# The negative maxima are issued ahead of the query and key stacks on SyncE's queue

## The chip, the cores and the metric

One core of a Trainium2 chip runs the kernel. The metric is the device time of one execution in microseconds (us); less is better. The median of three runs is shown together with the lowest and highest.

## The reference

An input x of 8 sequences of 1,024 positions by 256 channels goes through one attention layer with 16 heads of 16 channels, in which a query sees only itself and the 128 positions before it, and then through a linear layer whose weights are replaced by their signs. Both have a layer norm (without gain) ahead and a residual around them.

```python
def attn(x):                                   # x is the layer norm of the input
    q = (x @ Wq.T + bq).reshape(B, S, 16, 16)  # k and v the same way
    scores = einsum('bqhd,bkhd->bhqk', q, k) * 0.25
    scores = where((j <= i) & (j >= i - 128), scores, -10000.0)
    p = softmax(scores, axis=-1) + 1e-9
    return einsum('bhqk,bkhd->bqhd', p, v).reshape(B, S, 256) @ Wo.T + bo
x = x + attn(layernorm(x))
x = x + layernorm(x) @ sign(weight).T
```

## The kernel before

Each of the 8 sequences is cut into 8 tiles of 128 positions, and two tiles make a pair. One slot of the main loop handles one tile's scores, and beside them, in software pipelining, other steps for tiles ahead and behind; `parts(b, t)` (L201) says which: `nm` is two tiles ahead, `mx` three ahead, `xr` two behind, `op` three behind, `ff` four behind; `k` (in even slots) is the pair that starts four tiles ahead, `ks` (in odd slots) the pair that starts one tile ahead. There are 64 slots and four short ones behind them. Below, "slot 24" is the 24th from 0, and t is its number within its sequence (slot 24 has t = 0, slot 25 has t = 1).

For the softmax the kernel finds an upper bound for each query row and head with cheap bf16 products: `max_scores` (L986) multiplies `q_stack` by `k_max` on TensorE into the tile `mx`, `row_max` (L716) reduces it on VectorE into `nmax` (negated), `turn_max` (L1019) transposes that on TensorE, `nmax_part` (L552, L558) copies it on ScalarE to `nmax_t`, and `stack_nmax` (L285) sends it by DMA into two rows of `q_stack`, where it is multiplied by a row of ones in `k_stack` and so is subtracted from the scores. `scores` (L1027) is the fp32 product of `k_stack` and `q_stack`, in 8 groups f of two heads (L1050), and `exp` (L536) takes the exponentials on ScalarE.

The stacks are built by DMAs inside SBUF, all on SyncE's queue: `stack_q` (L243) sends a pair's queries in six DMAs of 128 KB (parts hi, hi, lo, each for two row groups, L256), `stack_k` (L269) a pair's keys in six DMAs of 128 KB (L282), `set_k_max` (L259) the bf16 keys in two DMAs of 64 KB (L266). `load_xr` (L292) fetches the residual's input and waits for `x2_done` of the slot before, `load_x` (L237) a pair of input tiles, and the output goes out at L317.

What waits for these DMAs on TensorE, which works in its own fixed order:

- `scores(b, t, 0)` waits for `nmax_stacked` of tile t + 1 (at t = 0 of tiles 0 and 1; at t = 7 of none), in even slots also for `k_stacked` of the slot's pair.
- `max_scores(..., 0)` waits, for an even tile, for `q_headed` (the first two query DMAs) and `k_max_set` (both of L266) of its pair. This tile is three ahead, so the wait falls into odd slots, one slot after the DMAs were issued.

In an odd slot TensorE's order is: `turn_max`, `scores` f = 0, `t1` (where there is a pair), `turn_u`, `turn_x2`, `scores` f = 1, then `max_scores` 0, and the rest. In an even slot SyncE's order is `load_xr`, `stack_q` three times, `stack_nmax`, `set_k_max`, output; in an odd slot `load_xr`, `stack_k`, `stack_nmax`, `load_x`, output. `stack_nmax` waits for `nm_done`, which L558 sets. `set_k_max` waits for `k_16_done`, the bf16 copy of the keys on ScalarE.

Of the kernel before, what the change touches and what calls it, by code (L numbers as in the profile page):

```python
# [45 lines left out]
def build(nc, x, wq_t, wk_t, wv_t, wo_t, wf_t, bq_c, bk_c, bv_c, bo_r, out):  # L46
# [7 lines left out]
    with ExitStack() as ctx:  # L54
# [132 lines left out]
        def wait(eng, s, n):  # L187

            if n > 0:
                eng.wait_ge(s, n)  # L190

        def halves(t):


            return t % 2, t // 2
# [5 lines left out]
        def parts(b, t):  # L201

            def tile(shift):
                bb, tt = b + (t + shift) // TILES, (t + shift) % TILES
                if not 0 <= bb <= LAST:
                    return None
                return bb, tt

            def pair(shift):
                n = t + shift  # L210
                if n % 2:
                    return None
                bb, pp = b + n // TILES, n // 2 % PAIRS
                if not 0 <= bb <= LAST:
                    return None
                return bb, pp

            if b > LAST:
                now = None
            else:  # L220
                now = (b, t)
            return now, {"nm": tile(2), "mx": tile(3), "pv": tile(-1), "xr": tile(-2), "op": tile(-3), "ff": tile(-4),
                         "tqv": pair(5), "k": pair(4), "ks": pair(1), "ln": pair(6), "load": pair(7)}

        def run(eng, slot):

            for b in range(BATCHES):
                for t in range(TILES):
                    slot(b, t)
            for t in range(4):  # L230
                slot(BATCHES, t)
# [3 lines left out]
        @block.sync  # L235
        def _(sp):
            def load_x(b, p):  # L237
                i, n = halves(p)

                wait(sp, xn_done, PAIRS * b + p - 1)  # L240
                sp.dma_start(xs[:, i], x_pair[b, p]).then_inc(x_loaded[i], 16)

            def stack_q(b, p, r):  # L243
                i, _ = halves(p)
                cols = slice(2 * P * p, 2 * P * (p + 1))
                g = PAIRS * b + p
                src = (q_hi, q_hi, q_lo)[r]
                stacked = q_stacked[i] if r else q_headed[i]

                wait(sp, sc_filled, SC_FILLS * (TILES * (b - 1) + 2 * p + 2))  # L250
                if g < PAIRS:
                    sp.wait_ge(q_zeroed, 1 if g == 0 else 2)
                sp.wait_ge(q_lo_done if r == 2 else q_hi_done, g + 1)
                for c in range(C):
                    at = 64 * c + DK * r
                    sp.dma_start(q_stack[at:at + DK, :, cols].bitcast(F32),  # L256
                                 src[:, g % 2, c, :].bitcast(F32)).then_inc(stacked, 16)

            def set_k_max(b, p):  # L259
                i, _ = halves(p)  # L260
                g = PAIRS * b + p

                wait(sp, mx_filled, MXG * (TILES * (b - 1) + min(2 * p + 3, TILES)))
                sp.wait_ge(k_16_done, g + 1)
                for c in range(C):
                    sp.dma_start(k_max[64 * c:64 * c + DK, :, P + 2 * P * p:P + 2 * P * (p + 1)],  # L266
                                 k_16[:, c, :]).then_inc(k_max_set[i], 16)

            def stack_k(b, p):  # L269
                i, _ = halves(p)  # L270
                g = PAIRS * b + p
                cols = slice(2 * P * (g % 2), 2 * P * (g % 2 + 1))

                wait(sp, sc_filled, SC_FILLS * (2 * g - 2))
                if g < 2:
                    sp.wait_ge(k_zeroed, g + 1)
                sp.wait_ge(k_hi_done, g + 1)
                sp.wait_ge(k_lo_done, g + 1)
                for c in range(C):
                    for r, src in enumerate((k_hi, k_lo, k_hi)):  # L280
                        at = 64 * c + DK * r
                        sp.dma_start(k_stack[at:at + DK, HB * c:HB * (c + 1), cols].bitcast(F32),  # L282
                                     src[:, g % 2, c, :].bitcast(F32)).then_inc(k_stacked[i], 16)

            def stack_nmax(b, t):  # L285
                i, _ = halves(t)
                sp.wait_ge(nm_done, TILES * b + t + 1)
                at = 3 * DK
                sp.dma_start(q_stack[at:at + 65:64, :, P * t:P * (t + 1)].bitcast(F32),
                             nmax_t[:, i, :].bitcast(F32)).then_inc(nmax_stacked[i], 16)  # L290

            def load_xr(b, t):  # L292
                i, _ = halves(t)

                wait(sp, x2_done, TILES * b + t - 1)
                sp.dma_start(xr[:, i], x_tile[b, t]).then_inc(xr_loaded[i], 16)

            def slot(b, t):
                now, part = parts(b, t)
                if part["xr"]:  # L300
                    load_xr(*part["xr"])
                if part["k"]:
                    for r in range(3):
                        stack_q(*part["k"], r)
                if part["ks"]:
                    stack_k(*part["ks"])
                if part["nm"]:
                    stack_nmax(*part["nm"])
                if part["load"]:
                    load_x(*part["load"])  # L310
                if part["k"]:
                    set_k_max(*part["k"])
                if part["ff"]:
                    bb, tt = part["ff"]
                    i, _ = halves(tt)
                    sp.wait_ge(y_done, TILES * bb + tt + 1)
                    sp.dma_start(y_tile[bb, tt], x2[:, i]).then_inc(y_stored[i], 16)  # L317

            def stack_ones(i):

                sp.wait_ge(k_zeroed, i + 1)
                for c in range(C):
                    at = 64 * c + 3 * DK
                    sp.dma_start(k_stack[at:at + 1, HB * c:HB * (c + 1), 2 * P * i:2 * P * (i + 1)].bitcast(F32),
                                 ones[0:HB, :]).then_inc(ones_stacked[i], 16)

            load_x(0, 0)
            load_x(0, 1)
            for dst, src in ((bq, bq_c), (bk, bk_c), (bv, bv_c), (bo, bo_r)):
                sp.dma_start(dst[:, :], src).then_inc(b_loaded, 16)  # L330
            load_x(0, 2)
            stack_q(0, 0, 0)
            stack_q(0, 0, 1)
            set_k_max(0, 0)
            stack_q(0, 0, 2)
            sp.wait_ge(ones_done, 1)
            stack_ones(0)
            stack_k(0, 0)
            stack_q(0, 1, 0)
            set_k_max(0, 1)  # L340
            stack_nmax(0, 0)
            stack_q(0, 1, 1)
            stack_nmax(0, 1)
            stack_q(0, 1, 2)
            load_x(0, 3)
            stack_ones(1)
            run(sp, slot)
            for i in range(2):
                sp.wait_ge(y_stored[i], 16 * (NT // 2))
# [984 lines left out]
```

## Time and profile before

| | us |
|---|---|
| median of 3 runs | 728.42 |
| lowest and highest run | 723.81, 730.84 |
| profiled execution, its own time | 729.17 |
| its span in the trace | 727.4 |
| TensorE busy (PE) | 667.2 (92% of the span) |
| VectorE, ScalarE, GpSimd busy | 493.5, 484.9, 457.5 |
| SyncE's DMA queue, share of 16 engines | 63.0% |

All times in the trace are us from the start of the span. In a timeline a row gives start, length, engine, line and operation, the number of instructions merged in it, and in brackets the idle time before it with what ended it. PE is TensorE's matmuls, PEld its weight loads, SPq the DMA issues of SyncE. "DMA q_stack<-nmax_t" as the end of a wait means that the transfer's landing ended it; "issue" means that the profile shows nothing that did. In the table of DMA issues the last number is the median time from the start of the issue to the landing, where there is one.

### The profile page before, as it was taken

How to read it: one execution, taken by the hardware profiler on the slowest of the kernel's cores; microseconds unless marked ns; L12 is line 12 of the kernel's file. 1: busy time of each engine (PE TensorE's matmuls, PEld its weight loads, DVE VectorE, ACT ScalarE, POOL GpSimd, SP SyncE). 2: the span in 40 equal slices, each digit the busy share in tenths (PEclk: the TensorE clock that was granted, in tenths of full speed). 3: DMA queues.
4: the chain of work that ended last, by engine and by line, in shares of the span. 5: the costliest groups of instructions: out<-in, count | busy, mean ns of one | idle time of the engine just before them, and what ended most of it. 6: DMA issues, size and time to landing. Idle time of an engine off the chain costs nothing.

```text
span 727.4 us, 31464 instructions
## 1 busy us (share of the span) xinstructions
PE 667.2 (92%) x13076; PEld 593.4 (82%) x13076; DVE 493.5 (68%) x1043; ACT 484.9 (67%) x1061; POOL 457.5 (63%) x650
## 2 busy tenths in 40 slices
PE   4579999999999999999999999999999999998874
PEld 4468888888988988888998888889888889887663
DVE  4544777777777777787677777677777777766434
ACT  4346777776767666777767677686767777675631
POOL 7924467766666667656666676475667666566652
PEclk9767999999999999999999999999999999999999
DMA  4957477876777676775767767675686757665401
GB/s 140 118 79 114 91 125 134 133 126 110 123 134 127 114 123 127 136 121 107 129 129 129 111 130 121 105 133 111 115 139 118 135 113 124 127 111 99 74 30 37
DMA packets 94940, 83.73 MB, mean 115 GB/s; under 512 B 10416, under 2 KB 94800, under 8 KB 94800
## 3 DMA queue, kind: packets, MB, share of 16 engines
q1 hardware_dynamic: 93440, 80.42, 63.0%
q8 instruction: 104, 1.70, 1.3%
q10 hardware_dynamic: 1360, 1.31, 0.5%
q14 instruction: 36, 0.29, 0.2%
HBM read 18.22 MB, written 8.39 MB: 37 GB/s over the span
## 4 chain that ended last, share of the span: by engine, by line
PE 77%; DMA 7%; DVE 5%; SPq 4%; issue 4%; ACT 2%; POOL 1%; DVEq 0%; ACTq 0%; POOLq 0%
PE gc L916 17%; PE sc L1050 16%; PE ga L916 12%; PE pv L1066 12%; DMA q_stack<-nmax_t 6%; PE mx L1007 5%; PE mx L1013 4%; PE ga L1076 3%; SPq L256 3%; DVE nmax L724 3%; PE gc L931 2%; PE gb L1105 2%; PE gb L1088 2%; ACT prob L548 1%; DMA k_stack<-k_hi 1%
## 5 line engine op out<-in xcount | busy, mean ns | idle before, releaser
L548 ACT ACTIVATE prob<-sc 128x512 f32<-128x512 f32 x448 | 259.2, 598 | 99.2 <-PE sc L1050 95.4
L724 DVE TENSOR_REDUCE nmax<-mx 128x6 f32<-128x960 f32 x189 | 197.1, 1043 | 75.6 <-PE mx L1013 74.4
L1050 PE MATMUL sc<-q_stack,k_stack 128*128 128x256 f32 (+1 forms) x1024 | 210.2, 305 | 8.9 <-DMA q_stack<-nmax_t 4.6
L1050 PEld LDWEIGHTS sc<-q_stack,k_stack 128*128 128x128 f32 x1024 | 150.6, 191 | 24.0 <-DMA q_stack<-nmax_t 7.2
L432 POOL TENSOR_SCALAR ve<-mv 128x1 f32<-128x1 f32 x64 | 14.2, 222 | 215.5 <-DVE mv L796 213.9
L419 POOL TENSOR_SCALAR_AFFINE_SELECT prob<-prob 128x1024 f32<-128x1024 f32 x128 | 139.8, 1092 | 0.0
L416 POOL TENSOR_SCALAR_AFFINE_SELECT prob<-prob 128x1024 f32<-128x1024 f32 x112 | 122.3, 1092 | 17.8 <-ACT prob L548 17.8
L1066 PE MATMUL pv<-prob,v_ones 128*32 128x128 f32 x3840 | 120.2, 277 | 1.0 <-POOL prob L419 0.7
L1066 PEld LDWEIGHTS pv<-prob,v_ones 128*32 128x32 f32 x3840 | 102.3, 111 | 10.2 <-POOL prob L419 1.0
L1013 PE MATMUL mx<-k_max,q_stack 16*32 16x160 bf16 x4032 | 72.0, 231 | 5.2 <-issue 5.2
L762 DVE TENSOR_TENSOR ct_lo<-gb,ct_hi 128x256 fp32r<-128x256 f32 x64 | 26.9, 420 | 45.1 <-ACT ct_hi L565 44.7
L1007 PE MATMUL mx<-edges,ident 32*32 32x192 bf16 (+1 forms) x1328 | 44.9, 246 | 10.8 <-DVE nmax L724 6.1
L1013 PEld LDWEIGHTS mx<-k_max,q_stack 16*32 16x32 bf16 x4032 | 44.7, 91 | 7.5 <-issue 6.1
L1007 PEld LDWEIGHTS mx<-edges,ident 32*32 32x32 bf16 x1328 | 18.8, 88 | 37.3 <-issue 15.0
L784 DVE TENSOR_TENSOR x<-ga,xr 128x256 f32<-128x256 f32 x64 | 27.2, 425 | 30.6 <-PE ga L916 29.4
L427 POOL TENSOR_TENSOR xr<-xr,brow 128x256 f32<-128x256 f32 x64 | 46.9, 732 | 0.0
L408 POOL TENSOR_TENSOR vsum<-vsum,v_ones 128x256 f32<-128x256 f32 x56 | 41.1, 734 | 2.5
L579 ACT ACTIVATE u<-pv 128x512 f32<-128x512 f32 x64 | 38.9, 608 | 5.6 <-PE pv L1066 5.5
L550 ACT ACTIVATE prob<-sc 128x256 f32<-128x256 f32 x64 | 23.7, 387 | 28.4 <-PE sc L1050 28.4
L504 ACT ACTIVATE q_hi<-gc,bq 128x256 fp32r<-128x256 f32 x64 | 26.8, 470 | 19.4 <-PE gc L916 16.8
L1076 PE MATMUL ga<-ident,u 128*128 128x128 f32 x256 | 38.7, 273 | 0.8 <-DVE x L784 0.8
L434 POOL TENSOR_TENSOR rs<-ve,half 128x1 f32<-128x1 f32 x64 | 36.0, 563 | 5.3
(149 smaller groups left out, 1409.2 us busy)
## 6 DMA issues: line engine op xcount, KB each, us to landing
q_stack<-q_hi SPq DMA_DIRECT2D x128, 128.0 KB, 3.6
k_stack<-k_hi SPq DMA_DIRECT2D x128, 128.0 KB, 4.4
xs<-x SPq DMA_DIRECT2D x32, 256.0 KB, 4.5
q_stack<-q_lo SPq DMA_DIRECT2D x64, 128.0 KB
k_stack<-k_lo SPq DMA_DIRECT2D x64, 128.0 KB, 4.2
xr<-x SPq DMA_DIRECT2D x64, 128.0 KB, 2.0
out<-x SPq DMA_DIRECT2D x64, 128.0 KB, 2.1
k_max<-k SPq DMA_DIRECT2D x64, 64.0 KB, 3.4
```

The costliest lines, as they stand in the source:

```text
L408: g.tensor_tensor(s, s, v, ALU.add).then_inc(vsum_step, 1)
L416: g.affine_select(out=nxt, in_=nxt, compare_op=ALU.is_ge, fill=0.0, base=0, pattern=[[0, HB], [-1, P]], channel_multiplier=1)
L419: g.affine_select(out=own, in_=own, compare_op=ALU.is_ge, fill=0.0, base=0, pattern=[[0, HB], [1, P]], channel_multiplier=-1).then_inc(pro ...
L427: g.tensor_tensor(xr[:, i], xr[:, i], brow[:, :], ALU.add).then_inc(xb_done, 1)
L548: a.activation(prob[:, own:nxt + 1:nxt - own, 2 * f:2 * f + 2, :], sc, ACT.Exp, scale=SCALE).then_inc(exp_done, 1)
L724: v.tensor_reduce(nmax[:, n % 2, :].rearrange("p (r h) -> p r h", r=C)[:, :, h0:h0 + m], banks[:, :, 0:WIN * m].rearrange("p r (h k) -> p ...
L916: last = mm(dst, l, r, start=j == 0, stop=j == len(terms) - 1)
L1007: mm(dst, ident16[rows, rows], mask.unsqueeze(1).broadcast_to(list(dst.shape)), start=True, stop=False, skip_group_check=True)
L1013: last = mm(banks[QB * blk:QB * (blk + 1), rg, WIN * j:WIN * (j + 1)], q_16[64 * rg:64 * rg + DK, h, at:at + QB], k_max[64 * rg:64 * rg + ...
L1050: last = mm(sc_bank[f % 2][:, 2 * P * j:2 * P * j + q], k_stack[:, h, ak:ak + P], q_stack[:, h % HB, P * t:P * t + q], start=True, stop=True)
L1066: last = mm(pv_bank[32 * j:32 * (j + 1), P * cg:P * (cg + 1)], v_ones[:, tile, h, :], prob[:, part, h, :], start=cg == 0 and k == 0, stop= ...
L1076: last = nc.tensor.transpose(ga[:, P * cg:P * (cg + 1)], u[:, t % 2, P * cg:P * (cg + 1)], ident[:, :])
```

## The change

In `slot` of SyncE's program the call of `stack_nmax` moves from behind `stack_q` and `stack_k` to the place in front of them, behind `load_xr`. No instruction is added or removed, and the part ahead of the loop keeps its order.

```diff
                 if part["xr"]:
                     load_xr(*part["xr"])
+                if part["nm"]:
+                    stack_nmax(*part["nm"])
                 if part["k"]:
                     for r in range(3):
                         stack_q(*part["k"], r)
                 if part["ks"]:
                     stack_k(*part["ks"])
-                if part["nm"]:
-                    stack_nmax(*part["nm"])
                 if part["load"]:
                     load_x(*part["load"])
                 if part["k"]:
```

## Rows read from the trace of the kernel before

**Rows 1.** The page: busy time of the engines.
```profile
PE 667.2 (92%) x13076; PEld 593.4 (82%) x13076; DVE 493.5 (68%) x1043; ACT 484.9 (67%) x1061; POOL 457.5 (63%) x650
```
**Rows 2.** Waits: who waited for whom, total us, times, longest us.
```profile
PEld mx L1007 <- issue: 16.4, 61, 2.6
PEld sc L1050 <- DMA q_stack<-nmax_t: 7.2, 12, 1.0
```
**Rows 3.** Timeline, SyncE's DMA issues in slots 24 (even) and 25 (odd).
```profile
294.25 0.33 SPq L296 DMA_DIRECT2D xr<-x  x1
294.69 2.54 SPq L256 DMA_DIRECT2D q_stack<-q_hi  x4
297.32 1.20 SPq L256 DMA_DIRECT2D q_stack<-q_lo  x2
298.57 0.55 SPq L289 DMA_DIRECT2D q_stack<-nmax_t  x1
299.97 1.60 SPq L266 DMA_DIRECT2D k_max<-k  x2
...
302.95 0.34 SPq L296 DMA_DIRECT2D xr<-x  x1
303.40 0.57 SPq L282 DMA_DIRECT2D k_stack<-k_hi  x1
...
307.19 0.60 SPq L282 DMA_DIRECT2D k_stack<-k_hi  x1
307.84 0.55 SPq L289 DMA_DIRECT2D q_stack<-nmax_t  x1
```
**Rows 4.** Timeline, TensorE at the start of slot 25.
```profile
303.23 0.51 PE L1050 MATMUL sc<-q_stack,k_stack 128*128 128x256 f32 x2 [0.42 <-DMA q_stack<-nmax_t]
...
304.99 0.28 PE L1007 MATMUL mx<-edges,ident 32*32 32x192 bf16 x8
```
**Rows 5.** DMA issues at 303.40 and 307.19, the first and last key DMA: to landing.
```profile
k_stack<-k_hi SPq DMA_DIRECT2D x1, 128.0 KB, 3.2
...
k_stack<-k_hi SPq DMA_DIRECT2D x1, 128.0 KB, 4.7
```
**Rows 6.** DMA issues: the second k_max of slots 24, 38, 20, 2, in this order.
```profile
k_max<-k SPq DMA_DIRECT2D x1, 64.0 KB, 3.6
k_max<-k SPq DMA_DIRECT2D x1, 64.0 KB, 4.6
k_max<-k SPq DMA_DIRECT2D x1, 64.0 KB, 3.8
k_max<-k SPq DMA_DIRECT2D x1, 64.0 KB, 2.3
```
**Rows 7.** Timeline, slots 38 and 39 (t = 7): k_max issues, TensorE's mx.
```profile
446.47 1.19 SPq L266 DMA_DIRECT2D k_max<-k  x2
...
451.79 0.28 PE L1007 MATMUL mx<-edges,ident 32*32 32x192 bf16 x8 [1.02 <-issue]
```
**Rows 8.** Timeline, slot 7, the first with t = 7: TensorE's mx.
```profile
119.36 0.28 PE L1007 MATMUL mx<-edges,ident 32*32 32x192 bf16 x8 [0.29 <-issue]
```
**Rows 9.** Timeline, slots 20 and 21 (t = 5): k_max issues, TensorE.
```profile
258.87 1.20 SPq L266 DMA_DIRECT2D k_max<-k  x2
...
261.90 0.51 PE L1050 MATMUL sc<-q_stack,k_stack 128*128 128x256 f32 x2 [0.76 <-DMA q_stack<-nmax_t]
...
263.66 0.40 PE L1007 MATMUL mx<-window,ident 32*32 32x480 bf16 x8
```
**Rows 10.** Timeline, ScalarE's copies of the maxima in slots 2 and 25.
```profile
68.49 0.25 ACT L558 ACTIVATE nmax_t<-gb 16x128 fp32r<-16x128 f32 x1
...
303.23 0.25 ACT L558 ACTIVATE nmax_t<-gb 16x128 fp32r<-16x128 f32 x1
```
**Rows 11.** Timeline, slots 2 and 3: SyncE's issues, TensorE's mx.
```profile
63.95 2.83 SPq L256 DMA_DIRECT2D q_stack<-q_hi  x4
...
73.35 1.58 SPq L266 DMA_DIRECT2D k_max<-k  x2
...
78.37 0.28 PE L1007 MATMUL mx<-edges,ident 32*32 32x192 bf16 x8
```
**Rows 12.** Timeline, TensorE's first scores of slots 16 and 26.
```profile
211.00 0.71 PE L1050 MATMUL sc<-q_stack,k_stack 128*128 128x256 f32 x4 [0.37 <-DMA k_stack<-k_hi]
...
313.48 0.72 PE L1050 MATMUL sc<-q_stack,k_stack 128*128 128x256 f32 x4
```

## The prediction

> **What bounds the kernel now.** I read the page first: TensorE is busy for 92% of the span and no other engine for more than 68% [rows 1]. So a change pays if it takes idle time out of TensorE's order, and costs if it puts some in. The waits view comes next: TensorE's weight loads stood 7.2 us, in 12 longer waits, until a DMA of negative maxima had landed [rows 2]. These are the first scores of odd slots. Slot 25 shows one: the DMA is issued at 298.57, behind six query DMAs, and the scores start at 303.23, 4.66 us later [rows 3, 4]. Slots with t = 7 have no such wait in the program, and in even slots the maxima are issued 5.6 us ahead of their use (307.84, scores at 313.48 [rows 3, 12]). So 7.2 us is what this order costs at that place; it is what the change can take away.
>
> The second place to look at is the next thing that an odd slot waits for: `max_scores` 0, behind f = 1, waits for `k_max`, which stands at the end of the same queue. In slot 39 the second `k_max` DMA is issued at 446.47 + 0.60 = 447.07 and takes 4.6 us to land, 451.7; TensorE starts `mx` at 451.79 after 1.02 us idle, labelled "issue" [rows 6, 7]. That label hides a DMA wait. The same reading holds in 6 of the 7 slots with t = 7 from slot 7 on (the first idles 0.29 us [rows 8]): there `mx` starts within 0.1 us of the landing. In the slots in which the maxima's wait comes first, `mx` starts soon after `k_max` landed: slot 25 at 304.99 against 300.57 + 3.6 = 304.2, a margin of 0.8; slot 21 at 263.66 against 259.47 + 3.8 = 263.3, a margin of 0.4 [rows 3, 4, 6, 9].
>
> **The queue is bound by its transfers, not by its issues.** SyncE issues a 128 KB DMA every 0.6 to 0.75 us. The key DMAs of slot 25 land at 303.40 + 3.2 = 306.6 (first) and 307.19 + 4.7 = 311.9 (last) [rows 3, 5]: five more DMAs in 5.3 us, 1.05 us each, about 125 GB/s. The query chain does the same, and `k_max` comes at its end: 304.2, which is 9.5 us after the first query issue (the median over the sequence of slots, read in this way, is 9.65). With the queue empty `k_max` needs 2.3 us from its second issue (slot 2, where the queries had gone long before) [rows 6, 11]; in slot 24 it needs 3.6. It stands 1.3 us behind transfers, so its landing follows the start of the chain, not its own issue. The Trainium skill, SBUF — State Buffer, section on the DMA port swizzle, says that bandwidth goes by how many of the 16 ports the partitions reach; 16 destination partitions reach four, an estimate of 109 GB/s and 1.2 us for such a DMA. The trace's 1.05 us is near that.
>
> **The change, part by part.** Nothing is added or removed; one DMA moves past six.
>
> 1. The maxima's DMA in even slots. It takes 0.55 us to issue and about 0.07 to the next: 0.62. ScalarE's copy is done when `load_xr` has been issued in the even slots (0.5 us to spare), so it waits for nothing and lands some 2.5 us after the slot's start instead of in the next slot. The waits at f = 0 vanish: at most 7.2 us gained.
>
> 2. The query chain starts 0.62 us later, so `k_max` lands 0.62 us later. I take the full 0.62, from the 1.05 us per DMA; the bounds are 0 (if the chain were issue-bound, since `k_max` is issued as before) and 0.62. Per odd slot TensorE gains the smaller of its f = 0 stall and (margin of `mx` behind `k_max`, less 0.62), which can be negative. Slot 25: stall 0.63, margin 0.76, gain 0.14. Slot 21: stall 0.96, margin 0.31, a loss of 0.31. Summed in this way over the 28 odd slots 5 to 59, for the bound 0 and for 0.62:
>
> | slots with | f = 0 stalls | gain, shift 0 | gain, shift 0.62 |
> |---|---|---|---|
> | t = 1 (7 slots) | 1.5 | +1.5 | +0.4 |
> | t = 3 (7) | 0.7 | +0.7 | 0.0 |
> | t = 5 (7) | 5.0 | +3.4 | -0.8 |
> | t = 7 (7) | 0 | 0 | -4.0 |
>
> The last line is what matters: with t = 7 there is nothing to gain, and `k_max` is already the wait, so six slots pay 0.62 and one pays 0.24.
>
> 3. The key chain in odd slots starts 0.62 us later, and up to 0.5 more where ScalarE's copy comes late: in slot 25 it ends at 303.48, when the first key DMA was issued at 303.40 [rows 3, 10]. Queued behind that wait are the six key DMAs, `load_x` and the output. The late copies (0.5) are in slots with t = 3, whose key landings have 2.7 us in hand. Elsewhere it is thin: 1.6 us in slot 26 (311.9 against 313.48 [rows 3, 5, 12]), none in slot 16, where the scores already wait for a key DMA [rows 12], and none in slot 50. Less 0.62, and less what the slot before gained, this costs 0.9 us at shift 0.62 (slots 42 and 50) and 1.6 us at shift 0.
>
> 4. The start. In slot 2 the queries are issued at 63.95, while the maxima are ready at 68.74 [rows 10, 11]: the chain starts 5.4 us later, at 69.4, and `k_max` lands at 69.4 + 9.65 = 79.0, against `mx` at 78.37 [rows 11]: 0.7 us lost. The waits in slots 0, 1 and 3 are covered by margins above 1 us, but for slot 1's `mx`, by 0.5.
>
> Sum: +0.4 + 0.0 - 0.8 - 4.0 - 0.9 - 0.7 = -6.0, so 6.0 us slower. The profiled execution's own time is 729.17, so 735.2; it stands 0.75 above the median 728.42, and against the median it is 734.4.
>
> **The rivals.** (a) The chain isn't work-conserving: `k_max` lands when it did, because it is issued when it was. Then 5.6 us are gained at f = 0, 1.6 lost to keys, none at the start: -4.0, so 724.4. For it speaks that the two DMAs' issues don't move, and that in slots whose fifth query issue came a microsecond late, the queries still all landed 8.9 us after the first issue. Against it: those had a backlog before them, and landings 1.05 apart are a full queue. The whole of 7.2 would come only if `k_max` were also ahead; the margins of 0.3 to 0.8 exclude it. The Trainium skill, DMA: Bandwidth & Descriptors, Anatomy of one DMA, fits a DMA at 2.0 us plus bytes over 436 GB/s: an estimate of 0.3 us for each 128 KB, by which the chain would be issue-bound and this rival right. The 1.05 us speaks against that here. (b) The shift is about half, 0.3: the same sum gives 0.0, and with the start 0.7 slower, 729. (c) SyncE gets stuck: one more DMA is outstanding ahead of the queries, SyncE's long issues (1.58 and 1.60 for two [rows 3, 11]) multiply, and `k_max` and the keys come a further 0.15 us late. With 28 odd slots that is 4 us more, 738.5; it decides once `k_max` lands over 0.75 us later. (d) The change doesn't do what it says: the maxima still land late. Only a late ScalarE copy could do that, and it isn't late in even slots.
>
> **How the numbers follow.** Full shift, 734.4: 0.50. Rival (a): 0.25. (b): 0.15. (c): 0.08. (d) and others: 0.02. The likeliest by itself spans 731 to 737. The range for 8 in 10 takes in (b), (c) and the upper part of (a): 724 to 738.5. About 1%, 7.3 us, is what a measurement can tell from no change. Faster by more than that needs all of the 7.2 us: 0.03. Slower by more than that needs (c) or the upper third of the first case: 0.25. Within 1%: 0.72.
>
> **What would show it.** The waits of TensorE for the maxima's DMA vanish from odd slots' first scores. The idle time labelled "issue" ahead of L1007 at the first `mx` of odd slots grows by about as much and more, with `k_max` landing 10.1 to 10.3 us after the slot's first query issue would have been (9.5 to 9.7 after the issue itself). In slots with t = 7 that idle time is 0.6 longer. If `k_max` lands 9.0 us after the first query issue, rival (a) is right. A few first scores of even slots wait for key DMAs. The prediction is wrong if a gain shows at f = 0 and none of it is given back at `mx`.

## The result, and the profile after

| | before | changed |
|---|---|---|
| median of 12 runs each, us | 730.05 | 735.93 |
| lowest and highest | 723.81, 732.20 | 732.55, 741.51 |
| ratio, 95% interval | | 1.0115 (1.0087 to 1.0142) |
| profiled execution: its own time, span | 729.17, 727.4 | 741.51, 739.5 |

The changed kernel is 5.9 us slower by the medians and 8.4 by the ratio (0.0115 x 730). The profiled execution of the changed kernel happens to be the slowest of its twelve, so its span overstates the difference. A second profile of each kernel was therefore taken (below), and both stand in the tables of slots 4 to 59.

The page of the changed kernel: busy time of the engines. TensorE does the same work, 666 us, in a longer span; the difference is idle time, as in [rows 1].

```profile
PE 666.3 (90%) x13076; PEld 593.3 (80%) x13076; DVE 494.1 (67%) x1043; ACT 486.2 (66%) x1061; POOL 457.7 (62%) x650
```

Its waits (who waited for whom, total us, times, longest), to be set against [rows 2]. The 7.2 us for the maxima's DMA are gone. The idle time ahead of the first kind of `mx` matmul went from 16.4 to 32.0, and the idle time labelled "issue" ahead of the scores from 1.2 to 6.3.

```profile
PEld mx L1007 <- issue: 32.0, 71, 4.5
...
PEld sc L1050 <- issue: 6.3, 11, 1.0
```

The last of these in the kernel before:

```profile
PEld sc L1050 <- issue: 1.2, 4, 0.6
```

SyncE's issues in slots 24 and 25 of the changed kernel, the slots of [rows 3].

```profile
296.54 0.57 SPq L289 DMA_DIRECT2D q_stack<-nmax_t  x1
297.22 2.52 SPq L256 DMA_DIRECT2D q_stack<-q_hi  x4
299.84 1.20 SPq L256 DMA_DIRECT2D q_stack<-q_lo  x2
302.45 1.65 SPq L266 DMA_DIRECT2D k_max<-k  x2
...
305.44 0.34 SPq L296 DMA_DIRECT2D xr<-x  x1
305.99 0.57 SPq L289 DMA_DIRECT2D q_stack<-nmax_t  x1
306.67 0.57 SPq L282 DMA_DIRECT2D k_stack<-k_hi  x1
```

TensorE at the start of slots 25 and 26. The first scores of slot 25 (305.10) follow without a wait, where [rows 4] had 0.42 us. Those of slot 26 now wait: their keys were issued later.

```profile
305.10 0.48 PE L1050 MATMUL sc<-q_stack,k_stack 128*128 128x256 f32 x2
...
306.84 0.28 PE L1007 MATMUL mx<-edges,ident 32*32 32x192 bf16 x8
...
316.22 0.71 PE L1050 MATMUL sc<-q_stack,k_stack 128*128 128x256 f32 x4 [0.63 <-issue]
```

And a slot with t = 7, slot 39, with the second `k_max` issue of slot 38 (450.79) in the table of DMA issues: 450.79 + 4.6 = 455.4, and `mx` starts at 455.52 behind 1.01 us of idle time. That is no longer than before (1.02 [rows 7]): slot 38 is an exception. There `k_max` lands 11.70 us after the slot's start before the change and 11.69 after it. The second query DMA was issued 1.20 us behind the first before and 0.60 now (1.13 and 0.60 in the second profiles), so the chain had been late there already. Slot 7 shows the usual case: where [rows 8] had 0.29 us of idle time, the gap between weight loads is 0.88 us against 0.40 before.

```profile
455.52 0.27 PE L1007 MATMUL mx<-edges,ident 32*32 32x192 bf16 x8 [1.01 <-issue]
```
```profile
k_max<-k SPq DMA_DIRECT2D x1, 64.0 KB, 4.6
```

The same readings over all slots, from the issues, landings and weight loads of the traces. "Start" of a slot is the weight load of its `turn_max`; the medians are over slots 4 to 56 (27 even slots, or the odd ones behind them), in us. "2nd" is the second profile of the same kernel.

| | before | 2nd | changed | 2nd |
|---|---|---|---|---|
| first query issue behind the even slot's start | 1.18 | 1.18 | 1.79 | 1.79 |
| k_max landed, behind the first query issue | 9.66 | 9.61 | 9.62 | 9.69 |
| k_max landed, behind the even slot's start | 10.84 | 10.79 | 11.41 | 11.48 |
| first key issue behind the odd slot's start | 0.93 | 0.96 | 1.75 | 1.74 |
| keys landed, behind the first key issue | 8.65 | 8.73 | 8.88 | 8.88 |

And TensorE's idle time in slots 4 to 59, summed by place from gaps above 0.15 us ahead of the first weight load of each:

| us | before | 2nd | changed | 2nd |
|---|---|---|---|---|
| first scores, odd slots (maxima) | 7.2 | 7.2 | 0 | 0 |
| first mx, odd slots (k_max) | 3.1 | 3.4 | 13.9 | 14.0 |
| first scores, even slots (keys) | 0.8 | 1.1 | 4.5 | 3.9 |
| length of slots 4 to 59 | 580.6 | 579.6 | 587.5 | 585.2 |

The three places together grew by 7.3 and 6.2 us, the slots by 6.9 and 5.6. One thing beside the waits adds to the 6.9: in the first profile of the changed kernel TensorE's granted clock was at half for 3.4 us from 666.9 on, in slot 59, which lasts 12.4 us against 10.4 and 10.9 before and 11.0 in the second profile.

### The profile page after: what moved, and what is told of

It reads as the page before. It is cut to its first block, busy times and chain, and to the rows that moved or that the text cites. A ratio compares the mean times of both kernels' runs of the same rounds, so it can differ in the third digit from the quotient of the medians.

```text
span 739.5 us, 31464 instructions
## 1 busy us (share of the span) xinstructions
PE 666.3 (90%) x13076; PEld 593.3 (80%) x13076; DVE 494.1 (67%) x1043; ACT 486.2 (66%) x1061; POOL 457.7 (62%) x650
## 4 chain that ended last, share of the span: by engine, by line
PE 84%; issue 5%; DVE 4%; POOL 2%; ACT 2%; DMA 1%; SPq 1%; POOLq 0%; DVEq 0%; ACTq 0%
PE gc L916 18%; PE sc L1050 17%; PE pv L1066 15%; PE ga L916 13%; PE mx L1007 6%; PE mx L1013 5%; PE ga L1076 4%; DVE nmax L724 2%; PE gb L1105 2%; PE gb L1088 2%; PE gc L931 2%; DMA q_stack<-q_hi 1%; PE gb L1025 1%; SPq L282 1%; ACT prob L548 1%
## 5 line engine op out<-in xcount | busy, mean ns | idle before, releaser
L1066 PEld LDWEIGHTS pv<-prob,v_ones 128*32 128x32 f32 x3840 | 103.4, 112 | 10.5 <-issue 1.2
L1007 PE MATMUL mx<-edges,ident 32*32 32x192 bf16 (+1 forms) x1328 | 44.6, 244 | 20.1 <-issue 13.8
```

The lines of the kernel that those rows point to most:

```text
L1007: mm(dst, ident16[rows, rows], mask.unsqueeze(1).broadcast_to(list(dst.shape)), start=True, stop=False, skip_group_check=True)
L1066: last = mm(pv_bank[32 * j:32 * (j + 1), P * cg:P * (cg + 1)], v_ones[:, tile, h, :], prob[:, part, h, :], start=cg == 0 and k == 0, stop= ...
```

## The experiments

Each was timed in turns with the kernel before on the same chip; "of before" is the ratio with its 95% interval. Two theories are tested: H, the head of the chain of transfers (what is put ahead of the queries delays `k_max`, their last link), and rivals that put the cost elsewhere. All diffs are against the kernel before, in SyncE's `slot`, unless it is said otherwise.

### The change in even slots alone

```diff
+                if part["nm"] and t % 2 == 0:
+                    stack_nmax(*part["nm"])
                 if part["k"]:
...
                 if part["ks"]:
                     stack_k(*part["ks"])
-                if part["nm"]:
+                if part["nm"] and t % 2:
                     stack_nmax(*part["nm"])
```

> The maxima go ahead of the stack only in even slots (ahead of the queries); in odd slots they stay behind the keys. Theory H (head of the chain): what costs is that the query chain starts 0.62 us later in even slots and k_max, its last link, lands 0.62 us later; so k_max lands 9.5 to 9.8 us after the first query issue as before, the first mx of odd slots idles as long as in the changed kernel, and the time is 4 to 5.5 us above before. The first scores of even slots wait for keys no more than in the kernel before (0.8 us in all). Rival K (the keys): the cost is in odd slots, where the key chain starts late; then this kernel is 3 to 5 us faster than before, since the waits for the maxima are gone.

Measured: 737.81 us, 1.0111 of before (1.0065 to 1.0156), 8.1 us slower; slots 4 to 59 last 586.5 us, 5.9 more than before. `k_max` lands 9.57 us after the first query issue and 11.34 after the slot's start. The waits view of this kernel (two lines lower in the file):

```profile
PEld mx L1009 <- issue: 34.4, 76, 3.8
```

The first `mx` idles even longer than in the changed kernel, and the keys' waits are gone (the only one above 0.15 us is 0.35 in slot 24). The gap there sums to 15.8 us in slots 4 to 59. So H holds for the waits, and rival K, which had this kernel faster, falls. By the timed runs this half is as slow as the whole change. How much of that is waiting, this profile cannot say. The waits at the three places grew by 5.1 us, but TensorE's clock was also at half for 6.8 us in slot 15 and for 3.4 in slot 59. These two slots last 15.0 and 12.8 us against 10.5 and 10.4 before, and without them the others are 0.9 us shorter than before (0.8 longer than in its second profile), although the waits grew: gaps inside groups of matmuls ("What the runs showed" below) are 1.9 us less, and the rest of that difference is open. The first of the two stretches (start and end, length, busy time of PE, PEld, DVE, ACT and POOL, granted clock, DMA share and rate):

```profile
205.60:212.40 6.80, 6.80 (x111) 6.05 (x109) 2.62 (x5) 1.77 (x5) 1.74 (x2) 0.50 0.77 101
```

### The change in odd slots alone, twice

```diff
+                if part["nm"] and t % 2:
+                    stack_nmax(*part["nm"])
                 if part["k"]:
...
                 if part["ks"]:
                     stack_k(*part["ks"])
-                if part["nm"]:
+                if part["nm"] and t % 2 == 0:
                     stack_nmax(*part["nm"])
```

> The maxima go ahead of the stack only in odd slots (ahead of the keys); in even slots they stay behind the queries. Theory H: the waits for the maxima at the first scores of odd slots stay (about 7 us), the key chain starts 0.62 to 1.1 us later, and some first scores of even slots wait for keys: 1 to 2.5 us slower than before. Rival K: all of the change's loss is here, 8 us or more slower than before (the change's 6 and the gain that is missing).

Measured: 738.08 us, 1.0111 of before (1.0075 to 1.0148). The waits view:

```profile
PEld sc L1052 <- issue: 9.2, 13, 2.2
...
PEld sc L1052 <- DMA q_stack<-nmax_t: 6.8, 11, 1.1
```

The maxima's waits stay, as H said, and the scores' waits labelled "issue" are the keys': the gaps there grew from 0.8 to 5.0 us. But the whole is 8 us, not 1 to 2.5. Since the profile put only 2.7 of these into slots 4 to 59 and 6.5 into the tail behind slot 60, it was run again:

> The kernel with the move in odd slots only, once more. Its first measurement lay 8 us above before, of which slots 4 to 59 account for 2.7 and the tail from slot 60 on for 6.5 in the profiles. If the tail's part belongs to the execution and not to the kernel, this profile's tail is between 59 and 66 us again at random and slots 4 to 59 last 583 us within 2; if the keys' waits alone cost what was measured, the first scores of even slots wait for 6 to 8 us again and the ratio is above 1.007.

Measured: 735.47 us, 1.0094 of before (1.0061 to 1.0127). Slots 4 to 59 last 585.5 us (4.9 more than before, so 583 within 2 was missed by half a us), the keys' gaps are 4.2 us, the tail 61.6. The timed runs put the odd part at 7 to 8 us by itself, but the two profiles find only 2.7 and 4.9 of these in slots 4 to 59, and of those 2.7 and 1.5 in the slots (34 and 35, and 41) in which the clock was at half for 3.4 us. The keys' gaps grew by 4.2 and 3.4. The rest lies in a tail that varies, and its cause is open. The six runs of each measurement had a mean granted clock of 0.970 and 0.974, the kernel before beside them 0.974 and 0.977. In the 49 executions of the kernel before that were timed beside these experiments, time falls by 4.4 us for each 0.01 of clock (correlation -0.80), so the clock may account for some 1.5 to 2 us of the 7 to 8, as an estimate. Neither half of the change was measured as harmless, and the two do not add. That the keys have time to land where `k_max` holds an odd slot up is a likely reason, which was not tested.

### Two profiles more: does the tail belong to the kernel?

> The kernel before once more, for a second profile. The question is the tail, from slot 60 to the end: 59.1 us in the profile of before and 64.2 in the changed kernel's, with 7 and 24 us at half of TensorE's clock. If the tail depends on the execution and not on the change, this profile may show any tail between 59 and 65 us, and slots 4 to 59 last 580 us within 3.

> The changed kernel once more, for a second profile. Slots 4 to 59 last 587 us within 3; the tail between 59 and 65 us. If it is the change that lengthens the tail, it is above 63 again.

Measured: before 730.26 us, slots 4 to 59 in 579.6, tail 62.3; changed 736.35, 585.2, 62.9. With the first profiles the tails are 59.1 and 62.3 against 64.3 and 62.9, with 5, 18, 18 and 17 us of them at half of the full clock. (The 24 us of the expectation took in the 3.4 in slot 59.) Over all kernels run here it lies between 59.1 and 65.6, in no order that follows the place of the maxima. So the tail varies by as much between executions of one kernel as between the two kernels; in slots 4 to 59 the change stands out, with 6.9 us in the first pair of profiles, slot 59 and its half clock included (4.9 without that slot), and 5.6 in the second (5.5 without it).

### The maxima behind two query DMAs

```diff
                 if part["k"]:
-                    for r in range(3):
-                        stack_q(*part["k"], r)
+                    stack_q(*part["k"], 0)
+                    stack_nmax(*part["nm"])
+                    stack_q(*part["k"], 1)
+                    stack_q(*part["k"], 2)
                 if part["ks"]:
                     stack_k(*part["ks"])
-                if part["nm"]:
+                if part["nm"] and not part["k"]:
                     stack_nmax(*part["nm"])
```

> In even slots the maxima stand behind the first two query DMAs and ahead of the other four; in odd slots they stay behind the keys. SyncE issues as many DMAs ahead of k_max as in the changed kernel, but the chain of transfers starts as early as in the kernel before, and by the third issue it has a backlog (1.05 us to land one, 0.64 to issue one). Theory H: k_max lands as in the kernel before (median 9.65 us after the first query issue), the maxima land 4 to 6 us after it, ahead of their use, and the time is 3 to 5 us below before. Rival C (SyncE's queue itself clogs, whatever the order): same as the changed kernel or at most 1 us better, 5 to 6 us above before.

Measured: 716.14 us, 0.9790 of before (0.9739 to 0.9842): 15 us faster by the ratio, the fastest kernel here (13 by the medians). SyncE's issues in slots 24 and 25, and TensorE at the start of slot 25:

```profile
286.88 1.24 SPq L256 DMA_DIRECT2D q_stack<-q_hi  x2
288.16 0.55 SPq L289 DMA_DIRECT2D q_stack<-nmax_t  x1
288.81 1.21 SPq L256 DMA_DIRECT2D q_stack<-q_hi  x2
290.12 2.70 SPq L256 DMA_DIRECT2D q_stack<-q_lo  x2
292.91 1.22 SPq L266 DMA_DIRECT2D k_max<-k  x2
```
```profile
294.86 0.47 PE L1052 MATMUL sc<-q_stack,k_stack 128*128 128x256 f32 x2
...
296.65 0.27 PE L1009 MATMUL mx<-edges,ident 32*32 32x192 bf16 x8
```

SyncE has issued as many DMAs ahead of `k_max` as in the changed kernel, and `k_max` lands 9.57 us after the first query issue and 10.75 after the slot's start, as before the change. The maxima land 3.3 us after their issue. The waits at f = 0 of odd slots are 0. That is H; rival C is out. Yet the gain is three times what H gave. Of the 13.8 us that slots 4 to 59 are shorter, 7.2 are the maxima's waits and 0.3 the keys'; the first `mx` idles 1.6 us more. That leaves 7.9 us, most of which is under "What the runs showed" below. Slot 4 also starts earlier, at 83.4 us against 87.7 and 86.4; in this profile the clock is full from 45.0 us on, where it was at half from 53.3 to 63.5 in the first profile of the kernel before. What brought that about was not tested.

### The maxima behind four query DMAs

The call stands one `stack_q` further back.

> In even slots the maxima stand behind four of the six query DMAs (two in the kernel measured before), in odd slots behind the keys. Theory H: once the chain has its head start, the place doesn't matter for k_max (10.7 to 10.9 us after the slot's start), and the maxima land 4 to 5 us after their issue, some 8.5 us after the slot's start, just ahead of their use: within 3 us of the kernel with the maxima behind two, 10 to 14 below before. Rival: each step further ahead costs a share, so this one lies halfway between that kernel and before.

Measured: 719.36 us, 0.9870 of before (0.9839 to 0.9901). That is 3.2 us above the kernel with two by the medians and 5.8 by the ratios, each to the kernel before in its own turn, so "within 3 us" was missed, and in time alone this kernel lies nearer to the rival's halfway. The trace speaks for H all the same: `k_max` lands 10.75 us after the slot's start again, and the waits view leaves 0.3 us for the maxima. For `k_max` only the head counts, as H says. Slots 4 to 59 last 572.2 us against 566.8; 5.3 of the 5.5 lie in slots with t = 0 and t = 2, where the waits for keys differ by 0.3 us; 3.8 of the 5.5 are the gaps inside groups of matmuls (below).

```profile
PEld sc L1052 <- DMA q_stack<-nmax_t: 0.3, 1, 0.3
```

### A second small DMA at the head

Against the changed kernel, whose call is the first one shown; the helper and its semaphore are left out here.

```diff
                 if part["nm"]:
                     stack_nmax(*part["nm"])
+                if part["k"]:
+                    spare_copy(PAIRS * part["k"][0] + part["k"][1])  # 8 KB of ones into a spare tile
```

> The changed kernel with one more DMA of the same size and shape (8 KB, ones into a spare tile) in even slots, between the maxima and the queries: the head of the chain moves by another 0.65 us. Theory H: k_max lands another 0.65 us later relative to the slot, every odd slot whose first mx already waits for it pays that in full (about 17 of 28) and the others in part: 9 to 12 us above the changed kernel, 15 to 18 above before. Rival A (k_max's landing follows its own issue, which another early DMA doesn't move): 0 to 1 us above the changed kernel.

Measured: 763.28 us, 1.0456 of before (1.0412 to 1.0499), 27 us above the changed kernel by the medians. The first query issue is 2.38 us behind the slot's start, `k_max` lands 9.70 after that, 12.10 behind the start: 0.69 more, as H says. The waits view:

```profile
PEld mx L1018 <- issue: 47.9, 82, 2.4
```

Rival A is out, but my size was far too small. The gaps at the first `mx` sum to 32.4 us against 13.9. 24 of the 28 odd slots have such a gap now, 15 in the changed kernel, so most of the slots whose margin had shielded them had none left; the rise is 0.66 us in the mean, from 0 in four slots to 1.5. On top, the granted clock fell to half for 6.8 us at 381, 470, 559 and 688 us. Slots 4 to 59 are 22.0 us longer than in the changed kernel, and 12.8 of these lie in the four slots of these stretches (31, 39, 47 and 59, 60.3 us against 47.4). In the 10 us ahead of each fall TensorE was busy for 8.3 to 8.6 us, and its longest gap in the 20 us ahead was 1.1 to 1.6 us. The changed kernel had one such stretch, of 3.4 us, in slots 4 to 59. That the longer idle time brought the others about is likely, but the kernel with the change in even slots alone also had one of 6.8 us, with half of this one's gaps at the first `mx`.

### The maxima on ScalarE's queue

SyncE's `slot` no longer calls `stack_nmax`; ScalarE's `nmax_part` issues the DMA for all tiles but the first two.

```diff
                 a.activation(nmax_t[:, i, :], gb[0:H, 0:P], ACT.Copy).then_inc(nm_done, 1)
+                if n > 1:
+                    act.wait_ge(nm_done, n + 1)
+                    act.dma_start(q_stack[...], nmax_t[:, i, :]...).then_inc(nmax_stacked[i], 16)
```

> In the main loop ScalarE issues the maxima's DMA itself, right behind the copy that fills nmax_t; SyncE's queue keeps everything else in the order of the kernel before, without the maxima. Theory H: the maxima land some 2 us after the copy, the query chain starts as early as in the kernel before (1.18 us after the slot's start) and k_max lands 10.8 us after the slot's start as before, so the time is near that of the kernel with the maxima behind two query DMAs: 10 to 15 us below before. Rival: the issue holds ScalarE up (0.5 us in each of 62 slots), the exponentials come late and TensorE waits for them: a gain of less than 5 us, or a loss.

Measured: 752.75 us, 1.0339 of before (1.0292 to 1.0385). The rival was right, and more so than it said. The chain is as H says (1.18, and `k_max` at 10.93), and the gaps at the three places sum to 1.2 us, but ScalarE takes 0.51 us for each issue and waits for its own copy ahead of it, at the start of the slot, where the exponentials follow one another. The issue in ScalarE's timeline, and the wait that it makes:

```profile
309.20 0.51 ACTq L560 DMA_DIRECT2D q_stack<-nmax_t  x1
```
```profile
PEld sc L1053 <- ACT prob L546: 34.7, 64, 1.4
```

In the changed kernel TensorE waited 4.2 us for these exponentials. ScalarE was busy for 66% of the span there, and still it was not free at this moment of the slot.

### The residual's load behind the stacks as well

On top of the kernel with two, `load_xr` moves from the head to behind `stack_nmax` of the odd slots and the stacks.

> The order of the kernel with the maxima behind the first two query DMAs (even slots) or behind the keys (odd slots), and besides the residual's load, with its wait for x2_done, at the end of that part and not at its head. Theory H: the chain of transfers now starts ahead of the wait, about 1 to 1.7 us earlier, and k_max and the keys land 0.7 to 1.5 us earlier, k_max then limited by ScalarE's bf16 copy; the waits at the first mx (4.7 us over slots 4 to 59 in the kernel with the maxima behind two) and at the keys (0.5) vanish: 3 to 6 us faster than that kernel, 16 to 20 below before. Rival: those waits are all that the order can give and the residual's load now comes late for GpSimd's sum, so that nothing is gained or 1 to 3 us lost against that kernel.

Measured: 721.03 us, 0.9910 of before (0.9875 to 0.9944): 5 us above the kernel with two by the medians, 9 by the ratios, where 3 to 6 less was expected. The first query issue is now 0.56 us ahead of the slot's start and `k_max` lands 9.94 behind it; the gaps at f = 0, for `k_max` and for the keys sum to 0.3 us. So the mechanism is there and the waits are gone, but slots 4 to 59 last 570.0 us against 566.8. Removing the last 4.9 us of DMA waits gave nothing; something else took 8 us of these slots (below). Neither theory had that right.

### The chain made shorter

In both orders the low part of the queries carries 32 of 256 columns from the third pair on; both kernels leave the low part of the other columns out of the scores.

```diff
+                    width = 32 if r == 2 and g > 1 else 2 * P
+                    cols = slice(2 * P * p, 2 * P * p + width)
                     sp.dma_start(q_stack[at:at + DK, :, cols].bitcast(F32),
-                                 src[:, g % 2, c, :].bitcast(F32)).then_inc(stacked, 16)
+                                 src[:, g % 2, c, 0:width].bitcast(F32)).then_inc(stacked, 16)
```

> The kernel before, but the two DMAs of the queries' low part carry 32 of 256 columns each from the third pair on (the low part of the other columns is left out of the scores). SyncE issues as many DMAs in the same order; the chain of transfers is 224 KB shorter, nearly 2 us. Theory H: k_max lands about 2 us earlier after the first query issue, no later than 9 us, the maxima behind the chain land 1.5 to 2 us earlier too, and the waits at f = 0 and at the first mx nearly vanish: 9 to 15 us below before. Rival S (what costs is SyncE's order and number of issues): within 3 us of before.

Measured: 716.97 us, 0.9835 of before (0.9794 to 0.9875). With as many issues, only fewer bytes, 12 us are gained: the place is bound by transfers. `k_max` lands 10.19 us after the slot's start, so the 2 us by which the chain is shorter show as 0.65. A `k_max` DMA now lands 2.7 us after its issue (3.4 before), near the 2.3 of an empty queue [rows 6]: it is near the limit of its own issue.

> The changed kernel with the same shorter low parts of the queries (the low part of the other columns is left out of the scores). Theory H: with a shorter chain k_max lands before it is needed in either order, so the change's cost in even slots is gone and only that of the keys in odd slots and of the start stays: 0 to 4 us above the kernel before with the shorter chain. Rival S: the change costs the same 6 to 9 us with the shorter chain as with the full one.

Measured: 721.96 us, 0.9913 of before (0.9880 to 0.9947); 5.0 above the other order with the short chain. The waits views of the two orders, the order of before first:

```profile
PEld sc L1052 <- issue: 1.6, 5, 0.5
```
```profile
PEld sc L1052 <- issue: 8.6, 16, 1.2
```

The gaps at the first `mx` sum to 1.6 us or less in both (13.9 with the full chain in the changed order), so `k_max`'s part of the loss is gone with its cause. What remains is the keys' part: their gaps are 7.0 us against 1.0. The whole difference is 5.0 us, above the 4 that I allowed. The keys' gaps grew more than in the changed kernel (6.0 against 3.7), perhaps because nothing else holds the odd slots up; that was not tested.

## Why the prediction was right, step by step

**What bounds the kernel; the transfers bind the queue.** Right. "Issue" ahead of `mx` was a DMA's landing, and shortening bytes without touching an issue gained 12 us.

**Step 1, the waits for the maxima.** Right: 7.2 us, all gone.

**Step 2, k_max lands 0.62 us later.** Right in the median: 0.61 at the first query issue, 0.57 to 0.69 at the landing. The first `mx` lost 10.8 us (10.6 in the second pair). Against the 7.2 gained that is a net 3.6 lost (3.4), where my table had 4.4 (0.4 gained at t = 1, 0.8 lost at t = 5, 4.0 at t = 7). Measured are 0.4 lost, 0.1 gained, 0.6 lost and 2.7 lost for t = 1, 3, 5 and 7. The table took the full shift for each slot with t = 7, but slot 39, from which the prediction read its example, had none: its chain already started late, with the second query DMA. Rival (a), a chain that is not work-conserving, and (b), a half shift, are excluded by the landing itself (0.57 to 0.69) and by the spare DMA: another 0.69.

**Step 3, the keys.** This is the term of the sum that was mis-sized. I gave 0.9 us; the gaps grew by 3.7 and 2.8 in the two pairs of profiles, and by 4.2 and 3.4 in the two profiles of the odd half by itself. I took the keys to come 0.62 us later and up to 0.5 more in slots with t = 3. Their first issue comes 0.82 us later in the median, and from it to the last landing takes 0.2 us more (8.65 to 8.88). The last keys land 0.9 us later behind the slot's start in the median (0.8 in the second pair), and seven even slots now wait for them (24, 26, 34, 42, 50, 52 and 54; six in the second profile), where I had counted two. The cause of the late first issue: the maxima's DMA can't be issued ahead of ScalarE's copy. In 18 of the 28 odd slots (19 in the second profile) SyncE now issues it 0.03 us after the copy's end, so it had waited for it, and the first key issue comes no earlier than 1.65 us behind the start in any slot (0.52 to 1.9 before). I had measured the wait against where SyncE stood in each slot of one profile.

**Step 4, the start.** Not seen: slot 4 starts at 87.7 and 86.4 us before, at 87.8 and 86.3 after. The wait named did come (slot 3's first `mx` idled 0.7 us more), and one that I had called covered but for 0.5 us came larger (slot 1's first `mx`, 1.9 and 1.7 us more). That the start came out even all the same was not foreseen, and what made up for them is open.

**The sum.** Forecast 6.0 us slower, 734.4; measured 5.9 by the medians, 8.4 by the ratio. The steps gave 5.3 for slots 4 to 59, and 6.9 and 5.6 were measured. The mechanism and the direction were right. That the sum came so near is in part luck: the keys' term was 1.9 to 2.8 us too small, the `k_max` term 0.8 to 1.0 too large, and the 0.7 of the start did not show. The chance for within 1% (0.72) was too high: by the ratio 1.15% lies just beyond, by the medians 0.8% lies within. The 2.5 us between medians and ratio are in no one place of the traces.

## What to carry to other kernels

In this queue, bound by its transfers, one small DMA at the head made the last link land 0.6 us later, and the same DMA behind two or four large ones made it no later. So try a small urgent DMA behind the first large ones (two was the best place here), not at the head and not at the end. Before a DMA is moved ahead, read who waits for the last link of that chain, and set idle time labelled "issue" against the landings of the DMAs that the instruction waits for. A DMA on another engine's queue costs that engine its issue (0.51 us of ScalarE here), and at the head of a slot that was on the path although the engine was idle for a third of the time. And before a difference of a few us is put down to a change, look for stretches of half clock: 3.4 or 6.8 us of it made the slots that it fell into 1.5 to 4.5 us longer here.

## What the runs showed of the hardware

TensorE has gaps in the middle of groups of matmuls that wait for no semaphore, above all in the third group of `max_scores` in slots with t = 0 and 2 (5.9 us of them in the kernel before). In the kernel before there are 9 above 0.3 us in slots 4 to 59, 8.9 us in all. All nine end 1.4 to 1.9 us after the end of a 16 KB transfer of the queue that the profile calls instruction, though these come only every 6.4 us. Nearly the same holds in the changed kernel (9 gaps, 7.8 us, eight of them so). Their sum is smallest with the maxima behind two query DMAs, 2.4 us, then 4.9 and 5.1 with the short chain, 6.2 behind four, and 9.0 with the residual's load late; two profiles of one kernel differ by 1.0 (before), 0.7 (changed) and 2.3 us (odd slots alone). So 6.5 of the 7.9 us that the kernel with two gained beyond the DMA waits lie here, and 6.6 of the 8 that the late load lost against it. That TensorE waits there for its instructions, whose transfer is held up by the stacks on the same DMA engines, is what these times suggest; it was not tested.

The granted clock fell to half inside slots 4 to 59 in six of the fourteen profiles, for 3.4 or 6.8 us at a time, though TensorE's longest gap in the 20 us ahead was only 0.5 to 1.6 us. Slot 15 took 15.0 us with 6.8 us at half clock (10.5 and 10.8 in the two profiles of the kernel before), slot 41 took 11.8 with 3.4 (10.3 and 10.2).

A DMA issued to 16 partitions (128 KB) lands every 1.05 us once the queue is full, while an issue takes 0.6 to 0.75. For 8 KB an issue takes ScalarE 0.51 us and SyncE 0.55 to 0.57.
